# Releasing every gather slot by a marker product in a graph-message kernel

## The reference: what is computed

```python
h = jnp.maximum(_layernorm(x, axis=-1), 0.0)             # x: (12500, 128) float32
# src, dst, edge_type: 200000 edges, sorted by dst; W: (4, 128, 128), b: (4, 128)
xs = h[src]
for i in range(4):
    mask = (edge_type == i)[:, None]
    msgs = msgs + jnp.where(mask, xs @ W[i] + b[i], 0.0)
out = x + jax.ops.segment_sum(msgs, dst, num_segments=12500)
```

## Time and profile before

| | |
|---|---|
| median of 3 runs | 2328.6 us (2311.18 to 2332.2) |
| the profiled execution, its own time | 2344.4 us |
| its span, first to last instruction | 2342.7 us |
| POOL busy | 1484.2 us (63%) |
| PE busy | 873.5 us (37%) |
| DVE busy | 705.6 us (30%) |
| ACT busy | 134.7 us (6%) |
| granted PE clock, mean | 0.652 of full speed |
| transfers | 144.73 MB, mean 62 GB/s |

### The profile page before, as it was taken

The page is one execution under the profiler, slowest core; times in us unless marked ns, Lnnn a source line. Parts: engine busy times, 40 slices in busy tenths (PEclk is TensorE's granted clock), DMA queues, the critical chain, the costliest instruction groups (busy, mean ns, idle before and its releaser), DMA issues.

```text
span 2342.7 us, 19295 instructions
## 1 busy us (share of the span) xinstructions
PE 873.5 (37%) x3921; PEld 641.9 (27%) x3922; DVE 705.6 (30%) x1734; ACT 134.7 (6%) x384; POOL 1484.2 (63%) x1573
## 2 busy tenths in 40 slices
PE   6774133233433343334343433343334233421233
PEld 2232122223322323222222232223222232321123
DVE  5554123233232323232323232323232233221123
ACT  3331000000000000000000000000000000000000
POOL 6666665756665666666666666666666666666763
PEclk8886566666665666666666665666666576665666
DMA  8663111111111111111111111111111111111231
GB/s 247 213 202 106 45 45 40 48 36 46 47 45 40 46 47 44 43 45 47 45 46 45 47 45 42 45 47 45 42 45 47 44 43 45 47 45 45 66 107 53
DMA packets 95454, 144.73 MB, mean 62 GB/s; under 512 B 27481, under 2 KB 57683, under 8 KB 95363
## 3 DMA queue, kind: packets, MB, share of 16 engines
q0 software_dynamic: 50016, 102.50, 16.8%
q1 hardware_dynamic: 40567, 38.92, 5.0%
q10 hardware_dynamic: 4780, 2.51, 0.4%
HBM read 111.73 MB, written 32.09 MB: 61 GB/s over the span
## 4 chain that ended last, share of the span: by engine, by line
another core or an unknown queue 29%; issue 25%; DVEq 24%; PE 10%; DVE 10%; ACT 1%; ACTq 0%; DMA 0%
DVEq L662 4%; PE ps_y L778 4%; DVEq L668 4%; DVEq L643 2%; DVE lists L643 2%; DVE acc L633 2%; PE ps_sum L828 2%; DVEq L633 2%; DVEq L625 2%; PE ps_y L857 2%; DVEq L655 2%; DVEq L663 2%; DVEq L672 2%; DVEq L271 2%
## 5 line engine op out<-in xcount | busy, mean ns | idle before, releaser
L369 POOL DMA_INDIRECT messages<-message_table,table_row x1155 | 1095.9, 949 | 613.3 <-issue 340.0
L828 PE MATMUL ps_sum<-messages,lists 128*128 128x128 f32 x1776 | 272.7, 320 | 570.3 <-DVE acc L633 341.5
L828 PEld LDWEIGHTS ps_sum<-messages,lists 128*128 128x128 f32 x1776 | 259.2, 233 | 581.8 <-issue 581.5
L369 POOL DMA_INDIRECT lists<-message_table,table_row x288 | 272.7, 947 | 147.2 <-issue 83.0
L672 DVE SCALAR_TENSOR_TENSOR ps_node<-node_iota,scaled_iota 128x128 f32<-128x128 f32 x200 | 72.3, 361 | 837.6 <-issue 825.9
L643 DVE SCALAR_TENSOR_TENSOR lists<-ps_node,node_iota,dst_col 128x512 f32<-128x512 f32 x296 | 212.6, 748 | 166.9 <-issue 131.0
L828 PE MATMUL ps_sum<-messages,onehot 128*128 128x128 f32 x582 | 116.8, 383 | 298.3 <-DVE acc L633 173.2
L828 PE MATMUL ps_sum<-lists 128*128 128x128 f32 x592 | 111.3, 366 | 222.8 <-issue 151.1
L828 PEld LDWEIGHTS ps_sum<-messages,onehot 128*128 128x128 f32 x582 | 110.8, 292 | 303.2 <-issue 303.2
L633 DVE SCALAR_TENSOR_TENSOR acc<-ps_sum,own_tile,acc x203 | 70.3, 346 | 357.1 <-remote 161.2
L828 PEld LDWEIGHTS ps_sum<-lists 128*128 128x128 f32 x592 | 106.4, 278 | 226.6 <-issue 226.6
(11 more groups left out here) (87 smaller groups left out, 524.5 us busy)
## 6 DMA issues: line engine op xcount, KB each, us to landing
message_table<-stage SPq DMA_DIRECT2D x98, 256.0 KB
messages<-message_table,table_row POOLq DMA_INDIRECT x1155
out<-acc SPq DMA_DIRECT2D x24, 256.0 KB
lists<-message_table,table_row POOLq DMA_INDIRECT x288
acc<-in_x SPq DMA_DIRECT2D x4, 896.0 KB
early_x<-in_x,src_col POOLq DMA_INDIRECT x119
acc<-in_x ACTq DMA_DIRECT2D x2, 896.0 KB, 6.0
acc<-in_x SPq DMA_DIRECT2D x1, 832.0 KB
```

Of the source, the lines that this page charges most:

```text
L369: pool.indirect_dma_start(messages[k][0:rows, t, :], None, table_rows, bass.IndirectOffsetOnAxis(ap=flat_rows[0:rows, at + t:at + t + 1], ...
L828: ins = nc.tensor.matmul(ps_sum[:, bass.ds(q % BANKS, 1), 0:d], onehots[k][:, t, :], messages[k][:, t, :], start=(t == 0), stop=(t == tile ...
```

## The change

PE frees every slot by the marker. `superblock` loses `frees`, the register `first_reg` and the wait L815/L816; the marker follows the products of each table superblock, the short one at the end excepted. With no slot of the round before to free, the first round behind the early part no longer needs a copy of its own ahead of the loop. Nothing changes on POOL, DVE, ACT and SP but line numbers.

```diff
--- before.py
+++ after.py
@@ -808,16 +808,10 @@
             pe.sem_inc(pair_done, LAG)
             pe.sem_inc(e_used, 1)
             pair_reg, pair = counter(pe, "pair", 1)
-            first_reg = pe.alloc_register("pe_first_pair")
             p_reg, early_count = counter(pe, "early_pair")
 
-            def pairs_done_since(signal):
-                pe.wait_ge(pair_done, pe.snap(first_reg, min_val=1, max_val=max_pairs + 1) + (LAG - 1))
-                pe.sem_inc(signal, 1)
-
-            def superblock(s, k, tiles, needed, frees, at_once=False):
+            def superblock(s, k, tiles, needed, release_slot=True):
                 windows, regs = load_windows(pe, s)
-                pe.reg_mov(first_reg, pair_reg)
                 with pe.Fori(0, windows):
                     q = pair()
                     pe.wait_ge(gathered[k], needed)
@@ -829,9 +823,7 @@
                                                    start=(t == 0), stop=(t == tiles - 1))
                         ins.then_inc(pair_done if half else first_half_done, 1)
                     pe.reg_add(pair_reg, pair_reg, 1)
-                if frees is not None:
-                    pairs_done_since(slot_free[frees])
-                if at_once:
+                if release_slot:
                     nc.tensor.matmul(ps_mark, release[:, 0:1], release[:, 0:1], start=True, stop=True).then_inc(slot_free[k], 1)
                 for r in regs:
                     pe.free_register(r)
@@ -871,19 +863,18 @@
                 for r in regs:
                     pe.free_register(r)
 
-            def table_round(i, first_frees, early_next=False):
+            def table_round(i):
                 for k in range(SLOTS):
-                    superblock(EARLY_SBS + i * SLOTS + k, k, SB_TILES, (i + 1) * (16 * SB_TILES), k - 1 if k else first_frees, early_next and k == SLOTS - 1)
+                    superblock(EARLY_SBS + i * SLOTS + k, k, SB_TILES, (i + 1) * (16 * SB_TILES))
 
             for a, z, keys in ((0, NARROW_ROUNDS, 2), (NARROW_ROUNDS, EARLY_SBS, SB_TILES // 2)):
                 with pe.Fori(a, z) as i:
                     for m in range(EARLY_ROUNDS):
-                        table_round(i * EARLY_ROUNDS + m, SLOTS - 1 if m else None, m == EARLY_ROUNDS - 1)
+                        table_round(i * EARLY_ROUNDS + m)
                     early_superblock(i, keys)
-            table_round(EARLY_SBS * EARLY_ROUNDS, None)
-            with pe.Fori(EARLY_SBS * EARLY_ROUNDS + 1, rounds) as i:
-                table_round(i, SLOTS - 1)
-            superblock(full_sbs, 0, last_tiles, rounds * 16 * SB_TILES + 16 * last_tiles, None)
+            with pe.Fori(EARLY_SBS * EARLY_ROUNDS, rounds) as i:
+                table_round(i)
+            superblock(full_sbs, 0, last_tiles, rounds * 16 * SB_TILES + 16 * last_tiles, False)
 
 
 # ---- launch: one core; inputs and outputs as the reference has them ----
```

## The result

The changed kernel takes 2301.1 us (median of 20 runs, 2279.4 to 2332.7) beside 2324.0 us for the kernel before (20 runs, 2310.1 to 2333.7): a ratio of 0.9884 with the interval [0.9862, 0.9906], 1.2% or 27 us faster (the ratio leaves out the slow executions, the medians, 23 us apart, do not). In a second comparison, experiment 9, it was 0.9881 [0.9842, 0.9920]. The forecast was 2317 us and 0.5%, with 2262 to 2360 as its outer range. The reason given for it is not the one that the experiments leave standing, nor is that rival's.

The account below looks back on a forecast made before the run. The prediction took POOL's run of gathers plus a stop that the others need to catch up as the bound. +3 - 9 - 6 = -12 us on the profiled 2344.4 us, scaled to a 2317 us median; range 2305 to 2345, outer 2262 to 2360.

Parts of the forecast that it names:

- The bound: POOL's unbroken gathers hold back PE's signals and slow DVE; a stop of some 4.4 us lets all catch up.
- The release itself, 0 us: POOL's refill waits: the marker's signal comes right behind the old one, so stops stay 4.4 us; 0 us gained.
- PE's lead, -9 us: Last rounds: PE, no longer shut out behind L816, runs ahead; cycles grow to four superblocks, -9 us.
- The mixed part, -6 us: Table and early superblocks: PE reaches the early superblock sooner, 0.5 us in each of 13 iterations, -6 us.
- The faster rival: PE's lead pays in the mixed part too: cycles of four superblocks everywhere, scaled 2269 us; chance 27%.
- The markers, +3 us: 165 more markers on PE at 0.164 us each, mostly hidden in idle time: +3 us, bounds 0 and 27.
- The slower rival: In POOL's run `pair_done` passes but the marker's signal is held until the stop, in 14 releases: scaled 2362 us; chance 18%.
- The rule on signals: Slots come free within a tenth of a microsecond of the product, POOL's 327.8 us of waits vanish: scaled 2003 us; chance 2%.

Follow-up runs that it names:

- experiment 9: The changed kernel unaltered, run once more against the kernel before: 2292.1 us, ratio 0.9881.
- experiment 2: Kernel before without PE's wait; the marker behind each superblock frees the slot of the one ahead of it: 2319.5 us, ratio 0.9987 to the kernel before.
- experiment 1: Changed kernel with PE's wait for the superblock ahead put back behind each marker: 2293.0 us, ratio 0.9896 to the kernel before.
- 10: Kernel before with its own marker only for slot 0 of the first round behind each early superblock but the last: 2305.6 us, ratio 0.9927.
- experiments 3: Changed kernel with PE's wait put back only ahead of each early superblock, 15 waits: 2306.6 us, ratio 0.9911 to the kernel before.
- 4: Changed kernel with PE's wait put back behind all table superblocks but the one ahead of each early superblock: 2298.0 us, ratio 0.9904 to the kernel before.
- experiment 5: Kernel before with its own marker only for slot 0 behind each early superblock but the last: 1976.2 us against 1975.0, ratio 1.0004.
- experiment 7: Changed kernel with a small POOL memset, waited for, ahead of each superblock's eight gathers: 1993.9 us, ratio 1.0096 to the kernel before.
- 8: Changed kernel with a small POOL memset, waited for, behind every gather: 2134.0 us, ratio 1.0804 to the kernel before.
- 11: Changed kernel with a small POOL memset, waited for, behind every gather, run once more: 2133.4 us, ratio 1.0801 to the kernel before.
- 12: Changed kernel with a small POOL memset, waited for, ahead of each superblock's gathers, run once more: 1993.5 us, ratio 1.0087 to the kernel before.

## Why the prediction was right and where it was wrong

**The bound** was read rightly for the condition that it was read from: the stops stay, most at 4.4 to 4.6 us of idle time, their sum is over 250 us, and DVE and PE go on being slow in POOL's runs. All three were named as what the profile would show. **That the forecast's outer range holds the result is luck**: +3, -9 and -6 us were added up for other causes than the one that makes the gain, and that one stood at 0.

**The release itself, 0 us,** is the step that failed. The own release is what the kernels with the gain share, 27 us in the changed kernel; experiment 2, which frees late, has nothing of it, and experiment 1, which gives the lead up, loses nothing that can be measured. I had looked at one cycle of the last rounds, where L816 waited for a signal and not for PE's program, and there the price is right: at a stop, L816 raises the slot's signal 0.09 us behind `pair_done` in the trace's records of the semaphores, the marker's signal comes 0.03 us behind it, and POOL goes on 0.26 us later in both. The full stops are 0.15 us shorter after (4.32 us on average beyond the step before, 4.18 after), but they are so in experiment 2 as well (4.15), without a gain. What I took for granted was the order of the stops, as if the same ones would come whatever the release. Eight stops of over 6 us were in the trace of before, seven of them for slot 0 right behind an early superblock, and the view of waits shows their presence as "longest 18.3". The mean of 4.97 us over 66 waits hid them.

A long stop is not the old release's own delay. Before, ahead of 971.18 (L816's row is from the window 960 to 972 us):

```profile
964.75 0.59 ACT L448 COPY bias<-ps_y 128x512 f32<-128x512 f32 x1 [72.23 <-remote]
965.68 2.07 PE L864 MATMUL ps_sum<-w_sb,bias 128*128 128x128 f32 x8 [12.96 <-ACT edge_counts L449]
967.98 2.84 PE L828 MATMUL ps_sum<-messages,onehot 128*128 128x128 f32 x16
...
L816 PEldq EVENT_SEMAPHORE  x1: 51/51/51, 970.9 to 970.9; - x1
```

The products that ACT's copies read had ended at 952.7 us, but the copies began only when POOL had stood for 3.8 us, and PE waited for the copies. Only then came the early superblock's last products and slot 0's, which ended at 970.8. So it is in all seven: PE begins L864 4.4 to 6.0 us ahead of POOL's next gather, in six of them after 11.7 to 21.5 us of waiting for ACT's copies, and L816 comes 0.1 to 0.2 us behind slot 0's `pair_done`. The changed kernel has one such stop left, with the marker and with the same wait of 13 us:

```profile
1622.06 2.07 PE L856 MATMUL ps_sum<-w_sb,bias 128*128 128x128 f32 x8 [13.02 <-ACT edge_counts L449]
1624.35 3.50 PE L822 MATMUL ps_sum<-messages,onehot 128*128 128x128 f32 x16
1627.77 0.16 PE L827 MATMUL ps_y<-ident 128*1 128x1 bf16 x1
1628.21 0.94 POOL L369 DMA_INDIRECT messages<-message_table,table_row  x1 [8.72 <-PE ps_y L827]
```

So it is the early superblock ahead of slot 0's products that makes these stops long, and the gain comes from such stops being rarer. Why they come mostly at every other early superblock before is my reading of the timelines: when slot 4's marker is heard in the middle of a run, POOL stops for only 2 us, and the signals of the early superblock are still on their way; the next stop must wait for those and for slot 0's own products. When slot 4's stop is a full one, everything is heard in it, and slot 0's is short. Experiments 1, 2 and 10 show that the second order repeats far more with the own releases. How a release that comes 0.06 us sooner at a stop does that is not shown. Nor is it tested whether another small shift in time, with the old release, would do the same.

**PE's lead, -9 us,** is refuted in size though its premise came true. PE does run the next superblock during POOL's run, but its products take until POOL's stop, and POOL's cycles in the last rounds stay mostly at three superblocks and 34.1 us. Runs of four don't occur in the changed kernel. In experiment 2 they do, five times, each ended by a stop of 6.7 to 14.4 us, as the one at 1069.13. **The mixed part, -6 us,** came out several times larger and from another cause, as above. The faster rival, the lead paying everywhere, has the same flaw, though the time lies in its range: experiment 1 gives the lead up and keeps 0.9896, and experiment 2 has all of the lead, with the later release, and 0.9987.

**The markers, +3 us,** can't be told from 0. In experiments 3 and 4 they are all there beside a gain of 0.9%.

**The slower rival,** one more signal held, is refuted. In the trace's records of the semaphores the marker's signal follows `pair_done` by 0.03 us at the end of a stop (1039.31 and 1039.34 us) and by 0.04 to 0.07 us in a burst (1051.20 and 1051.24, 1051.42 and 1051.49). In the middle of POOL's run signals do pass one by one, as the rival said, but the marker's mostly comes only 0.7 to 2.8 us behind (947.69 and 949.12, 983.33 and 985.45), and not at the next stop.

**The rule on signals** (the Trainium skill, TensorE: Matmul & The Clock Gate, The cost: per-tile semaphore tail, some 26 ns for each signal) had 2% and would have given 2003 us. In the comparison of experiment 5 the kernel before takes 1975 us, and in the profile of its sibling with one release changed the waits of the earlier trace rows are gone altogether, as that rule would have it, and with no help from the change. In experiment 7's profile each of the 180 markers is heard 0.18 us after it starts. The trace of one comparison could not have shown that. I wrote that the two always stand together, POOL's run and the slow phases, and that nothing separates them. The comparison of experiment 5 does: POOL's even run, at the same 1.249 us a gather, is not enough to slow the others. The signals are held in the comparisons on chips 4 and 3 (experiments 1 to 4, 9 and 10) and not in those on chips 8 and 9 (5 to 8, 11 and 12). Each chip was used in one comparison, so that it is the chip and not something else about the comparison isn't shown, and the cause stays open.

## What to carry to other kernels

List the longest waits one by one before pricing a wait at zero by its usual case: a mean over all of them hides the few in which something longer, here a whole early superblock, stands ahead of the release. In a ring with stops, ask which order of long and short stops repeats, and don't hold it fixed when a signal in the ring changes: here a release that is 0.06 us quicker at a stop went with another order and 1.2%. And a gain that comes out of stops exists only where the stops do: here it is 1.2% in the comparisons with them and, by the estimate of experiment 7, nothing in those without.

## What the runs showed of the hardware that I had not expected

- The same kernel before takes 2324, 2321 and 2321 us in three comparisons and 1975.0 and 1975.4 us in two on other chips, each with a spread of at most 1.4%. In the first three every profile has 68 to 72 stops of POOL; in the other two the kernels of experiments 5 to 8, 11 and 12 have none over 1.7 us.
- In the first kind of comparison the sixteen instructions of a superblock's products took 22 us in POOL's run, and a register instruction of DVE 0.70 us; in the second they take 3.78 us and 0.045 us beside the same gathers.
- POOL's even step is the same in both, 1.249 us, of which 0.94 us is the gather and 0.30 us the idle time in front of it. A memset of 128x8 with a wait for it adds only 0.092 us to that step, though it takes 0.118 us itself: the mean gap is partly free.
- The mean granted TensorE clock was 0.657 of full speed in the changed kernel's profile and 0.673 in that of experiment 5, so the clock does not explain the 15%.
